# Moving the products of weights, the transposes of x1 and the row sums in the first two steps of a batched graph kernel

## What is computed

```python
h = jnp.maximum(_layernorm(x, axis=-1), 0.0)
x = x + _L0_gnn_ref(h, adj, ...)      # hypergraph_conv, relu, layer_norm, hypergraph_conv, + h
h = jnp.maximum(_layernorm(x, axis=-1), 0.0)
x = x + _L1_gnn_ref(h, adj, ...)      # attention-weighted diffusion, 3 terms

def hypergraph_conv(x, adj, W, b):    # H = (adj != 0), w = first row of adj
    xw = jnp.einsum('ncd,hd->nch', x, W)
    Dn = jnp.einsum('nce,ne->nc', H, w);  Dn = jnp.where(Dn > 0, 1.0 / Dn, 0.0)
    Be = H.sum(axis=1);                   Be = jnp.where(Be > 0, 1.0 / Be, 0.0)
    m = Be[:, :, None] * jnp.einsum('nce,nch->neh', H, xw)
    return Dn[:, :, None] * jnp.einsum('nce,neh->nch', H, m) + b
```

## Time and profile before

| | us |
|---|---|
| median of 3 runs | 823.0 (822.75 to 823.59) |
| the profiled run | 824.4 |
| its span, first to last instruction | 822.6 |
| PE busy in the span | 806.7 |
| DVE busy | 641.9 |
| ACT busy | 475.3 |
| POOL busy | 425.6 |

### The profile page before, as it was taken

One profiled execution on the slowest core, in us unless ns is written; L12 is line 12 of the kernel. 1 busy time (PEld: TensorE's weight loads), 2 busy tenths in 40 slices (PEclk: granted clock), 3 DMA queues, 4 the chain that ended last, 5 costly groups with the idle time before them and its releaser, 6 DMA issues.

```text
span 822.6 us, 16660 instructions
## 1 busy us (share of the span) xinstructions
PE 806.7 (98%) x5750; PEld 753.2 (92%) x5750; DVE 641.9 (78%) x1738; ACT 475.3 (58%) x1005; POOL 425.6 (52%) x587
## 2 busy tenths in 40 slices
PE   7898999999999999999999999999999999999998
PEld 6787999999899998999999899998999999999997
DVE  5787887778788777887778788777887878786676
ACT  4347457483664737557383664737557483664745
POOL 2647473645827366383644836366382645832242
PEclk9899999999999999999999999999999999999999
DMA  9421204022050312305022040302204022020001
GB/s 295 127 65 52 90 2 163 6 78 90 0 166 0 122 44 61 104 0 166 0 76 89 6 160 0 128 37 71 95 0 166 0 76 89 16 89 1 26 2 52
DMA packets 39856, 57.83 MB, mean 70 GB/s; under 512 B 2576, under 2 KB 21008, under 8 KB 39824
## 3 DMA queue, kind: packets, MB, share of 16 engines
q1 hardware_dynamic: 39104, 57.42, 21.1%
q10 hardware_dynamic: 720, 0.01, 0.0%
HBM read 49.03 MB, written 8.39 MB: 70 GB/s over the span
## 4 chain that ended last, share of the span: by engine, by line
PE 90%; DVE 1%; ACT 0%; issue 0%; POOL 0%; DVEq 0%; POOLq 0%
PE ps L795 85%; PE ps L1007 3%; PE ps L937 2%; PE ps L983 1%; ACT xl L555 0%; DVE y L1205 0%; DVE x L1417 0%; DVE x L1210 0%; DVE part_a L1189 0%; DVE st_x L1423 0%; POOL rs_x L432 0%; DVE xt_lo L1216 0%; ACT r_sb L561 0%; DVE r_sb L1286 0%; ACT y_hi L588 0%
## 5 line engine op out<-in xcount | busy, mean ns | idle before, releaser
L406 POOL TENSOR_TENSOR y<-y,bk_row 128x256 f32<-128x256 f32 x64 | 56.6, 915 | 199.2 <-DVE a_lo L1316 190.3
L795 PE MATMUL ps<-w_hi,part_a 128*128 128x256 f32 (+1 forms) x512 | 156.8, 341 | 1.4 <-DVE part_a L1189 1.4
L795 PE MATMUL ps<-w_lo,part_a 128*128 128x256 f32 (+1 forms) x384 | 123.0, 320 | 0.0
L795 PEld LDWEIGHTS ps<-w_hi,part_a 128*128 128x128 f32 x512 | 96.7, 189 | 14.4 <-DVE part_a L1189 2.7
L795 PE MATMUL ps<-wk_hi,xt_hi 128*128 128x258 f32 (+1 forms) x256 | 89.1, 348 | 2.2 <-DVE xt_lo L1216 2.2
L795 PE MATMUL ps<-wk_hi,xt_lo 128*128 128x258 f32 (+1 forms) x256 | 86.7, 338 | 0.0
L795 PE MATMUL ps<-wk_lo,xt_hi 128*128 128x258 f32 (+1 forms) x256 | 86.6, 338 | 0.0
L795 PEld LDWEIGHTS ps<-w_lo,part_a 128*128 128x128 f32 x384 | 73.2, 191 | 5.7
L1310 DVE TENSOR_TENSOR e_sb<-e_sb,adjt_sb 128x512 f32<-128x512 f32 x64 | 44.5, 696 | 41.8 <-ACT e_sb L664 41.8
L795 PE MATMUL ps<-w_hi,part_b 128*128 128x256 f32 x256 | 72.7, 284 | 0.0
L470 POOL TENSOR_TENSOR xt_lo<-xl,xt_hi 128x256 fp32r<-128x256 f32 x60 | 56.7, 975 | 31.0 <-ACT xt_hi L738 31.0
(11 more groups left out here) (157 smaller groups left out, 2530.0 us busy)
## 6 DMA issues: line engine op xcount, KB each, us to landing
adj_sb<-in_adj SPq DMA_DIRECT2D x30, 512.0 KB, 5.9
adjt_sb<-in_adj_t SPq DMA_DIRECT2D x15, 1024.0 KB, 5.4
xin<-in_x SPq DMA_DIRECT2D x15, 512.0 KB, 4.6
out_dram<-x SPq DMA_DIRECT2D x15, 512.0 KB, 3.3
w_row<-in_adj SPq DMA_DIRECT2D x16, 256.0 KB, 3.4
adjt_sb<-in_adj_t SPq DMA_DIRECT2D x4, 256.0 KB, 7.3
e_sb<-in_w_t SPq DMA_DIRECT2D x2, 512.0 KB, 8.3
y<-in_wk SPq DMA_DIRECT2D x3, 256.0 KB, 6.9
```

The lines of the kernel that those rows point to most:

```text
L406: pool.tensor_tensor(y10[:, t, D:], y10[:, t, D:], bk_row[:, :], ALU.add).then_inc(po_y0, 1)
L795: return pe.matmul(dst, stationary, moving, start=first, stop=last, skip_group_check=True)
```

## The change

`products_of_weights` goes from behind `mean_of_beta` to between `y` and `g_stage` of step 0 and writes `ps0` instead of `ps1`; what ScalarE does with it goes behind the four `h_of`, save `c0_row`, which has a semaphore of its own. `w2_lo` goes from DVE to POOL, where the four skips of the first graph are split around it and around `rs_r`, and `bk_row` and the next graph's `xb` go behind `h_hi`. DVE's order in step 0 is rewritten: the incidence tiles stand later, x1 with its statistics stands ahead of `sums(2)`, and the shift of x1 ahead of `u_lo(1)`. In step 1 the transposes of x1 run ahead of z's third tile and write `ps1`. In step -1 the last block of `m_first` is interleaved and the counts are taken in pairs; `m_stage` of step 0 waits tile by tile.

```diff
+                    skip_of_first(2)
+                    skip_of_first(3)
                     rs_of_x(s)
...
+                    pool.tensor_tensor(bk_row[:, :], bk_f[:, 0, :], bk_f[:, 1, :], ALU.add).then_inc(su_rows, 1)
+                    pool.wait_ge(su_rows, 2)
+                    pool.tensor_tensor(bk_row[:, :], bk_row[:, :], bk_f[:, 2, :], ALU.add).then_inc(su_rows, 1)
+                    pool.wait_ge(su_rows, 3)
+                    xb_of_next()
...
+                    rs_of_part(Step(4, 1, 1, NB), TI, 1)
                     pool.wait_ge(su_wkhi, 1)
-                    wait(pool, dv_x1, at(s, 0))
+                    wait(pool, dv_hw, at(s, 1))
...
+                pool.wait_ge(su_w2hi, 1)
+                pool.tensor_tensor(w2_lo[:, :, :], w2_c[:, :, :], f32(w2_hi[:, :, :]),
+                                   ALU.subtract).then_inc(su_w2lo, 1)
+                skip_of_first(0)
+                skip_of_first(1)
...
-                    relu(1)
                     xt_of(0)
                     xt_of(1)
+                    relu(1)
...
-                        act.wait_ge(su_pe, 1)
-                        act.activation(c_e[:, :], ps1[:, 2, 0:1], ACT.Identity, bias=ab_c[:, :]).then_inc(su_c, 1)
-                        act.activation(c0_row[:, :], ps1[:, 0, 0:D], ACT.Copy).then_inc(su_c, 1)
-                        act.activation(wk_f[:, :, D:D2], ps1[:, 1, 0:2 * TD].rearrange("p (a b) -> p a b", a=TD),
-                                       ACT.Copy).then_inc(su_wk, 1)
-                        act.wait_ge(su_c, 1)
-                        act.activation(c_e[:, :], ps1[:, 2, 1:2], ACT.Identity, bias=c_e[:, :]).then_inc(su_c, 1)
+                        act.wait_ge(su_bet, 1)
+                        act.activation(c0_row[:, :], ps1[:, 0, 0:D], ACT.Copy).then_inc(su_c0, 1)
...
+                    act.wait_ge(su_w2lo, 1)
...
+                    act.wait_ge(su_pe, 1)
+                    act.activation(c_e[:, :], ps0[:, 2, 0:1], ACT.Identity, bias=ab_c[:, :]).then_inc(su_c, 1)
+                    act.activation(wk_f[:, :, D:D2], ps0[:, 1, 0:2 * TD].rearrange("p (a b) -> p a b", a=TD),
+                                   ACT.Copy).then_inc(su_wk, 1)
+                    act.wait_ge(su_c, 1)
+                    act.activation(c_e[:, :], ps0[:, 2, 1:2], ACT.Identity, bias=c_e[:, :]).then_inc(su_c, 1)
...
+                def second_transposes():
+
+                    for t in range(2):
+                        wait(pe, ac_xl, at(s, -1, 2 * t + 1))
+                        wait(pe, dv_x1, at(s, -1))
+                        for j in range(2):
+                            for d in range(TD):
+                                last = pe.transpose(ps1[:, t, col(2 * j + d)], xl[:, 2 * t + j, col(d)],
+                                                    ident[:, :])
+                        last.then_inc(pe_xt, 2)
...
+                        if s.k == 1 and t == 2:
+                            second_transposes()
...
                 if s.k == 0:
                     mean_of_beta()
-                    products_of_weights()
-                if s.prev:
+                if s.prev and s.k != 1:
...
-                        if s.here and t < 2:
+                        if s.here and (t < 2 or s.k == 1):
...
+                        pe.wait_ge(h_hi_made, i + 1)
+                        if i < TI - 1:
+                            for t in range(TI):
+                                mm(ps0[:, t, 0:D2], inc[:, o, i, col(t)], h_hi[:, i, :], i == 0, False)
+                        pe.wait_ge(h_lo_made, i + 1)
                         for t in range(TI):
-                            pe.wait_ge(h_hi_made, i + 1)
-                            mm(ps0[:, t, 0:D2], inc[:, o, i, col(t)], h_hi[:, i, :], i == 0, False)
-                        for t in range(TI):
-                            pe.wait_ge(h_lo_made, i + 1)
+                            if i == TI - 1:
+                                mm(ps0[:, t, 0:D2], inc[:, o, i, col(t)], h_hi[:, i, :], False, False)
                             last = mm(ps0[:, t, 0:D], inc[:, o, i, col(t)], h_lo[:, i, :], False, i == TI - 1)
                             if i == TI - 1:
                                 last.then_inc(pe_m, 1)
...
-                    wait(pe, dv_inc, at(s, 1))
-                    wait(pe, h_lo_made, at(s, 1))
...
+                            if s.k == 0 and t == 0:
+                                wait(pe, dv_inc, at(s, 1, i))
+                                wait(pe, h_lo_made, at(s, 1, i))
...
                 elif s.k == 0:
+                    pe.wait_ge(dv_ntlo, TI)
+                    products_of_weights()
                     g_stage()
+                    pe.wait_ge(su_c, 2)
+                    pe.wait_ge(su_wk, 1)
                     m_stage()
...
-                    wait(dve, pe_m, at(s, 1))
-                    dve.tensor_scalar(be_cnt[:, :], ps0[:, :, D], 1.0, None, ALU.max).then_inc(dv_bec, 4)
-                    dve.wait_ge(dv_bec, at(s, 1))
-                    dve.reciprocal(be[:, o, :], be_cnt[:, :]).then_inc(dv_be, 4)
                     inct_tile(1)
+                    for h in range(2):
+                        pair = slice(2 * h, 2 * h + 2)
+                        wait(dve, pe_m, at(s, 1, 2 * h + 1))
+                        dve.tensor_scalar(be_cnt[:, pair], ps0[:, pair, D], 1.0, None, ALU.max).then_inc(dv_bec, 2)
+                        dve.wait_ge(dv_bec, at(s, 1, 2 * h + 1))
+                        dve.reciprocal(be[:, o, pair], be_cnt[:, pair]).then_inc(dv_be, 2)
+                    inct_tile(2)
                     m_lo(0)
                     m_lo(1)
-                    inct_tile(2)
                     m_lo(2)
+                    inct_tile(3)
                     m_lo(3)
-                    inct_tile(3)
...
                     z_tile(2)
+                    z_tile(3)
                     stats_r(0)
-                    z_tile(3)
                     stats_r(1)
-                    dve.wait_ge(su_w2hi, 1)
-                    dve.tensor_tensor(w2_lo[:, :, :], w2_c[:, :, :], f32(w2_hi[:, :, :]), ALU.subtract).then_inc(su_w2lo, 1)
-                    incidence(0)
-                    incidence(1)
+                    stats_r(2)
...
+                    lo_of_nt(1)
                     lo_of_nt(2)
...
                     means_of_x(0, TI)
-                    lo_of_nt(3)
                     y_lo(0)
-                    incidence(2)
                     y_lo(1)
+                    incidence(0)
                     y_lo(2)
                     shift_of_x(0, TI)
+                    incidence(1)
                     y_lo(3)
+                    incidence(2)
+                    h_lo_of(0)
+                    dve.wait_ge(su_c0, 1)
+                    g_tile(0)
                     incidence(3)
-                    dve.wait_ge(su_c, 3)
-                    g_tile(0)
-                    h_lo_of(0)
+                    h_lo_of(1)
                     g_tile(1)
-                    h_lo_of(1)
-                    g_tile(2)
                     h_lo_of(2)
                     h_lo_of(3)
+                    g_tile(2)
...
+                    inct_of()
                     sums(0)
+                    m_parts()
                     sums(1)
-                    inct_of()
-                    m_parts()
+                    second = Step(4, 1, 1, NB)
+                    x1_tile(0)
+                    for t in range(1, TI):
+                        x1_tile(t)
+                        stats_x1(t - 1)
+                    stats_x1(TI - 1)
...
                     sums(2)
+                    u_lo(0, second)
                     sums(3)
-                    second = Step(4, 1, 1, NB)
                     sign_of_total(second)
+                    wait(dve, po_rsx, at(second, 1, 1))
+                    dve.scalar_tensor_tensor(nb_x[:, TI:], mv_x[:, TI:, 0], -1.0, rs_x[:, TI:],
+                                             ALU.mult, ALU.mult).then_inc(dv_nbx, 2)
+                    u_lo(1, second)
+                    safe_total(second)
                     stats_x(0, 2)
-                    safe_total(second)
+                    inverse_total(second)
                     stats_x(1, 2)
-                    inverse_total(second)
-                    stats_x(2, 2)
-                    stats_x(3, 2)
-                    for t in range(TI):
-                        x1_tile(t)
                     wait(dve, dv_x1, at(s, 0))
                     dn_of_total(second)
-                    u_lo(0, second)
-                    stats_x1(0)
-                    u_lo(1, second)
-                    for t in range(1, TI):
-                        stats_x1(t)
...
-                    dve.wait_ge(dv_st1, at(s, -1))
+                    z_tile(0)
+                    stats_x(2, 1)
+                    stats_x(3, 1)
+                    dve.wait_ge(dv_stx, at(s, 1))
                     dve.memset(landed_0[:, :], 0.0)
```

(62 more changed lines are left out.)

29 lines of the change are left out of this document (15 added, 14 removed).

## The result

| | before | changed |
|---|---|---|
| median, us | 822.74 (821.44 to 823.59, 6 runs) | 826.22 (825.87 to 827.16, 6 runs) |
| ratio to before | 1 | 1.0045 [1.0035, 1.0055] |
| profiled execution: run, span | 824.4, 822.6 | 825.9, 824.1 |
| its mean granted clock | 0.994 | 0.998 |

A forecast was written before the change was run, and what follows sets the result against it. TensorE, busy 98% of the span, was taken as the bound, with early waits and half clock to win. Gains of 0.65, 3.75 and 2.7 less 1.0 made 6.1 us: 823.0 to 816.9, called 817.0, range 814.8 to 819.7.

The forecast's parts named there:

- Term 2: Step 0, products of weights behind y: transposes at full clock, y ends at 37.9; 5.8 us won, not all let through.
- Term 1: Step -1, edge counts in pairs: u starts 0.3 us sooner, z 0.65; gain 0.65 us, bounds 0 and 2.0.
- Term 3: Load behind incidence(1) issued 6.7 us later: DVE idles, PE waits 2.2 us for h_lo; gain 3.75 us at u_lo(1).
- From there on the queues are the old ones: After si and its transposes: PE stays full, so no gain of the first steps is lost later.
- E: PE falls to half clock at the two-column matmuls behind y and stays there: 825 us or more, chance 0.02.
- F: Gain not had: another engine is as far behind, PE waits later in step 1; 822 to 824 us, chance 0.04.
- Rival C: Clock doesn't fall in u since the idle shrinks to 1.4 us; z 2.0 us sooner, 815.6 us, chance 0.18.
- Rival D: POOL's w2_lo takes 2.96 us or the load lands 1 us later, or both: 818 to 819.5 us, chance 0.12.
- The rule that I weighed and left out of the sum: POOL work beside the four h_lo tiles slows DVE: at 0.3 us longer each, the gain would be 4.9 us.
- Term 4: Transposes of x1 inside z: waits of 2.22 and 0.27 us go; gain 2.7 us, y2 ends at 68.1.
- Term 5: Given back after z(3): DVE still has 4.6 us of work until si at 70.5, PE waits 1.0 us.
- Rival B: Clock falls in the new waits, inside m or around z's start: 817.7 to 819.4 us, chance 0.22.

The follow-up runs named there:

- whole counts: Changed kernel with the first edge counts taken whole again, one maximum and one reciprocal, loop at instruction 278: 822.14 us, ratio 0.9999 to before.
- 821.90: Changed kernel with 64 one-column memsets at the head of VectorE's program, loop at instruction 346: 821.90 us, ratio 0.9997 to before.
- the last pair of kernels: Changed kernel with early incidences, shift behind u_lo(1), x sums behind g's splits, no memsets: 816.96 us with whole edge counts, 821.93 us with counts in pairs.
- kernel with both edits: Changed kernel with 32 memsets, first two incidences taken behind nt(1) and nt(2), and x1's shift behind the second u_lo: 820.41 us, ratio 0.9972.
- 817.57: Changed kernel with 32 memsets, early incidences, shift behind second u_lo, and GpSimd's four x sums behind g's splits: 817.57 us, ratio 0.9936.

## Why the prediction was wrong

**Step that failed first: the time I took the gains from.** Every term was an old moment less a new one, and the old moments came from an execution of 824.4 us whose clock was half for two stretches of the front. I named these 5 us of half clock and counted their absence as the change's work: of the 6.4 us by which Term 2 ends y sooner (44.31 to 37.9), the kernel before with four memsets has 3.95 without any of the change (40.36). Up to 76 us it is the same code but for the memsets, and in its profiled execution the clock did not fall in those two stretches, only once and later, from 67.2 to 70.6 us. Stretches of before as first profiled, then of before with four memsets, then of the changed kernel (us, busy, clock, DMA share, GB/s):

```profile
32.00:40.00 8.00, 7.82 (x41) 7.82 (x42) 3.92 (x12) 3.14 (x8) 5.07 (x9) 0.57 0.61 207
```

```profile
15.00:20.00 5.00, 4.57 (x17) 2.60 (x16) 4.72 (x11) 2.03 (x4) 0.00 (x0) 1.00 1.09 355
32.00:40.00 8.00, 7.22 (x60) 6.80 (x59) 6.93 (x24) 3.73 (x10) 5.07 (x8) 1.00 0.39 150
...
66.00:71.00 5.00, 3.31 (x17) 3.34 (x18) 4.11 (x9) 2.74 (x7) 0.76 (x2) 0.66 0.01 3
```

```profile
15.00:20.00 5.00, 4.40 (x18) 2.81 (x17) 4.65 (x11) 1.74 (x4) 0.00 (x0) 1.00 1.09 354
32.00:40.00 8.00, 8.00 (x69) 8.00 (x70) 5.11 (x18) 4.30 (x11) 5.59 (x10) 1.00 0.40 134
45.00:50.00 5.00, 4.60 (x25) 4.42 (x24) 4.64 (x12) 2.06 (x5) 4.34 (x5) 0.66 0.60 210
```

The moments, read from the orders of time:

| us | before, as profiled | before, four memsets | changed | whole counts |
|---|---|---|---|---|
| g starts | 44.31 | 40.36 | 37.49 | 37.63 |
| nt starts | 53.72 | 49.77 | 50.60 | 49.09 |
| second u_lo done on DVE | 62.8 | 58.88 | 61.05 | 60.43 |
| si made | 75.92 | 73.11 | 72.99 | 73.22 |

Against an undisturbed execution of the same code the change leads by 2.9 us at g, by 0.7 at nt if its own clock holds, trails by 1.6 to 2.2 at the second u_lo, and is even at si. Of the 6.1 us forecast at si (75.92 to 69.85, Term 1 taken in), 2.8 lay in the old moment (73.11 in the execution without the two stretches) and 3.1 in the new one (72.99). My new moments were about right until m; behind it DVE was later than I had it, by Term 3 below. The list of executions says the same: of 23 runs of before beside the whole counts, those with a mean clock of 0.998 took 821.4 to 822.5 us, those with 0.995 or 0.996 822.8 to 823.6, those with 0.993 or 0.994 824.2 to 824.5. The one I read was of the last kind, 1.4 us above the median by which I wrote it down, and 2 to 3 above its own floor.

**Step that failed second, and decided the sign**: "From there on the queues are the old ones, PE is full and nothing is lost." The queues are the old ones, but the loop stood four instructions further on, and each of five jumps cost DVE 3.6 us, of which 0.8 to 1.05 reached PE: 4.5 us in the trace; by the medians 4.3 (826.22 less 821.90) and 5.0 (821.93 less 816.96). I costed every instruction of Term 1 by its duration and none by its place. No rival had this mechanism. E, the one on the slower side, had another, and it did not come: behind the two-column matmuls the clock stayed at 1.00 until 46.1 us. F, whose 822 to 824 the kernel all but takes with the loop in a good place (821.9 to 822.1), was right that the gain isn't had in the first two steps, and had a chance of 0.04.

Term by term, by the rows:
- Term 1, counts in pairs: 0.65 with bounds 0 and 2.0. u began at 14.13 instead of 14.27 with whole counts, and z 0.12 us sooner; in the last pair of kernels both were some 0.5 sooner. Within the bounds, at their low side, and it was this term that added the four instructions.
- Rival C was right for u: the clock held (1.00 from 15 to 20 us). But it also held in the kernel before with four and with two memsets, after the same idle of 1.73 us. So the shorter idle was not needed for it.
- Term 2, products behind y: y ended at 36.24, earlier than my 37.9 less 0.65; w2_lo took 2.37 us on GpSimd, between the two prices. Right, but worth 2.9 us at g and not 6.
- Term 3, the load: its mechanism came out as written, 3.55 us of DVE, 3.1 of PE for h_lo against 2.2. The issue came at 36.86 and not at 38.0, but the landing took 4.1 us and not 3.4, which is what Rival D spoke of. Mis-sized was DVE's queue from the third incidence to the second u_lo: 16.8 us by my sum, 20.1 by the trace (40.98 to 61.05). Of that 1.64 us is the one shift, which took 1.79 us where 0.15 is usual. It ran beside GpSimd's split of wk, and ended when the first half of that split did:

```profile
58.65 1.79 DVE L1608 SCALAR_TENSOR_TENSOR nb_x<-mv_x,rs_x 128x4 f32<-128x4 f32 x1
60.37 0.68 DVE L1229 TENSOR_TENSOR part_a<-ps,part_a 128x512 fp32r<-128x512 f32 x1
...
58.61 3.32 POOL L498 TENSOR_TENSOR wk_lo<-y,wk_hi 128x770 fp32r<-128x770 f32 x2 [0.71 <-DVE hw L1208]
```

 The two halves took 1.81 and 1.55 us, so the first ended at 60.42 and the shift at 60.44.

 The rule that I weighed and left out of the sum spoke of this: by the Trainium skill (GPSIMD Engine Reference, 8. Key points) GpSimd contends with VectorE instructions that have two SBUF inputs. The trace agrees: the shift has two, while u_lo, with one of its operands in PSUM, kept its 0.68 us beside the same split. But I had the form of the price wrong, 0.3 us an operation beside the h_lo tiles. Such an operation lasts as long as the GpSimd operation beside it: with the shift behind u_lo (kernel with both edits) it started 1.0 us later into the same half of the split and took 0.80 us, to its end. The kernel before shows it in every step of its loop. The last product for dn, on 128x4 numbers, has a shortest, median and longest time of

```profile
L1277 DVE TENSOR_TENSOR dn<-dn_t x16: 161/683/687, 24.2 to 751.5; 128x4 f32<-128x4 f32 x16
```

 and the 13 of some 0.68 us all end 0.02 us behind the GpSimd sum that runs beside them, while the three without one already running take 0.16. So the 0.15 that I had for usual holds for a GpSimd at rest. The rest of the 3.3 us is by the rows some 0.8 us for the two incidence tiles (0.99 and 0.55 us where I had 0.7 for both) and a wait of 0.49 for ScalarE ahead of the first u_lo; what is left, some 0.3, I can't divide:

```profile
57.17 0.69 DVE L1229 TENSOR_TENSOR part_a<-ps,part_a 128x512 fp32r<-128x512 f32 x1 [0.49 <-ACT part_a L559]
```

- Term 4, transposes in z: the wait of 2.22 us is gone, as forecast. Term 5: 1.0 us for si, measured 1.38. Since DVE's queue ended later, both only moved the end of it.
- Rival B held in part: the clock fell once, in m, behind the waits for h_lo (0.66 from 45 to 50 us). It cost 1.5 us at nt (50.60 against 49.09 with whole counts, where it didn't fall there). si was made no later (72.99 against 73.22), but there the clock fell too, from 60.7 to 64.1 us, so that DVE bound at si, as I had said, is likely and not shown.

## What to carry to other kernels

Before taking an old moment from a trace, look whether that execution's clock and time are those of the fastest runs; a wait or a half-clock stretch that other executions of the same code don't have can't be won by a change. When a change adds instructions ahead of a loop, compare the time of one pass of the untouched loop first: a standstill named "issue" at its head, and more packets in the instruction queue, tell that it is the loop's place and not the change, and a few idle instructions more or fewer show it. Before an operation with two SBUF inputs goes ahead of something that TensorE waits for, look at what GpSimd does beside it. The new order, with three more edits and the loop in a good place, was worth some 6 us, and most waits that were taken away showed the next one on another engine.

## What the runs showed of the hardware that I had not expected

- A loop of 276 listed and 284 executed instructions on DVE ran without a fetch when it began at instruction 278, 280, 314 or 346 of its program. At 282 it took five packets of 8 KB and a standstill of 3.6 to 3.8 us at each jump back; at 306 there were two standstills, of 2.5 and 2.3 us, and the kernel took 833 to 840 us. An account that fits the starts, the number of packets and the times at which they come: DVE holds four packets of 128 instructions, fetches one ahead, and the loop must lie in three. How many it holds is worked out from these and not measured by itself.
- The Trainium skill (Runtime: NRT & Kernel Launch, Instruction fetch mechanics) says that a taken branch to instructions that aren't held forces a fetch before execution goes on; the trace agrees, with 3.6 us at each jump. It gives 512 instructions held for engines like this, in blocks of 256. Four packets of 8 KB would be that size, but they come one at a time and are half such a block. With two blocks held, the next of them fetched while one runs, no loop over two blocks would go free of fetches, and the loop of the kernel before, longer than one block, did from 182 to 699 us. The measurement decides.
- A DVE operation on 128x4 numbers with two SBUF inputs took 1.79, 0.80 or 0.68 us by how much of the GpSimd operation beside it was left, and 0.15 to 0.16 us beside none.
- Whether PE's clock fell in these first steps differed between executions of one kernel, by up to 3 us of its time. With the front's waits for h_lo and for the splits of g gone, 8 of 9 executions (817.57 and 816.96) had a mean clock of 0.999 or more, and the last four lay within 0.14 us of each other. With the same front and the loop in the bad place the clock was 0.999 or more in all nine that are compared, and yet they took 821.4 to 823.5 us: what the standstills cost differs between executions by itself.
